# Self-attention with kept score tiles: six kept steps of eight in place of five, and the work around them set to other steps

## The chip, the cores and the metric

The kernel runs on one core of one Trainium2 chip. The metric is device time in microseconds (us) of one launch; the figure shown for a kernel is the median of its runs. A profile is taken from one separate execution. The engines are TensorE (PE in the profile, its weight loads PEld), VectorE (DVE), ScalarE (ACT), GpSimd (POOL) and SyncE (SP), which issues all DMAs here.

## The reference, cut to what matters

Four images of 256 channels and 64 x 64 places (4096 columns) go through two layers. Layer 0 is group norm, then self-attention over the 4096 places, added to the input; layer 1 is group norm, a 1 x 1 convolution to 32 channels, all 528 products of pairs of these, and a 1 x 1 convolution back to 256, added again.

```python
f = einsum('kc,bcn->bkn', Wq, gn(x)) + bq      # 32 x 4096
g = einsum('kc,bcn->bkn', Wk, gn(x)) + bk      # 32 x 4096
h = einsum('oc,bcn->bon', Wv, gn(x)) + bv      # 256 x 4096
s = einsum('bki,bkj->bij', f, g)               # 4096 x 4096
beta = softmax(s, axis=1)
x = x + gamma * einsum('bci,bij->bcj', h, beta)
y = relu(bn(einsum('bchw,oc->bohw', gn(x), w1) + b1))          # 32 channels
z = relu(bn(einsum('bhwt,ot->bohw', y[rows] * y[cols], w2) + b2))
x = x + z
```

## The kernel before, in words

The attention is worked tile by tile. A tile is 128 keys (columns j of `s`); there are 32 tiles in an image and 128 in all. Each tile takes eight steps, one for each chunk of 512 queries, in the order of `CHUNK_AT`. A step of the program has the index `u`; `t` is its place in a group of four tiles (0 to 31), `J` the group in an image (0 to 7), `b` the image (0 to 3), `s8` its place in the tile (0 to 7). All numbers are split in a high and a low half of float16, so that a step on TensorE holds eight matmuls of the high half of the powers with both halves of `h` (L1772, L1773) and, at its end, four with the low half (L1784). In between stands the score piece of a tile that is `AHEAD` = 18 steps on (L1577): 128 keys by 512 queries, from which VectorE takes the maximum.

The powers `exp(s - max)` of a step come about in one of two ways.

- **Made in place.** TensorE computes the scores again, transposed, four matmuls of 128 x 128 (`scores`, L1597), two or three steps ahead. ScalarE takes the exponential twice from PSUM (`powers`: `ph`, float16, L1333, and back to PSUM in float32, L1334), VectorE subtracts the one from the other to give the low half (`low_part`, `pl`, L896).
- **Kept.** VectorE writes the score piece to SBUF while it takes its maximum (`ks`, L863). Once the tile's maximum is known (`tile_max`, `kbias`), ScalarE takes the exponential in place (L1345); the high half `kb` is either a second exponential by ScalarE (L1343, the places in `HIGH_BY_ACT`) or a cast by VectorE (L891); GpSimd subtracts to give the low half (`kept_low`, L1162). SyncE then issues a DMA transpose of both halves into `kt` (`turn`, L521), and TensorE takes `kt` as weights.

`KEPT_STEPS` says which of the eight steps of a tile are kept, from tile 2 on. For each of them, `EXP_AT`, `CAST_AT`, `LOW_AT` and `TURN_AT` say at which step ScalarE, VectorE, GpSimd and SyncE take their part of it into their own order; steps of 8 and more are those of the tile itself, smaller ones those of the tile before. Every engine runs its own program in order, and semaphores are all that ties them; the rings `ks`, `kb` and `kt` hold 8, 4 and 5 pieces.

The three banks of the score pieces and of the other small results are used in turn: a piece on TensorE waits until VectorE has read the one two steps earlier. When a tile is done, VectorE takes the reciprocal of its sum (`invert`, in step 1 of the next tile), ScalarE divides (`divide`, L1351, `ot`), and after four tiles TensorE transposes `ot` and VectorE adds it to x (`finish`). The rest of the work (normalising chunks for the queries, keys and values of the next image, `xh` on ScalarE, L1301; the second layer of the image before: `rt`, `ql`, `qh`, `zt`) stands at fixed places `t` in the same orders. x lies in a ring of `XR` chunks; a chunk that isn't there any more is loaded again through `xt`.

Of the kernel before, what the change touches and what calls it, by code (L numbers as in the profile page):

```python
# [33 lines left out]
KEPT_STEPS = (1, 2, 4, 6, 7)  # L34
# [20 lines left out]
XR = 14  # L55
# [8 lines left out]
def build(nc, x, wq, wk, wv, w1, w2, vec, ident, gmean, sel, out):  # L64
# [5 lines left out]
    with ctx:  # L70
# [130 lines left out]
        kp_ok, kc_ok, kl_ok = sem("kp_ok"), sem("kc_ok"), sem("kl_ok")  # L201
# [39 lines left out]
        VORD = (4, 0, 5, 1, 6, 2, 3, 7)  # L241
# [206 lines left out]
        def _(sp):  # L448
# [149 lines left out]
        def _(dve):  # L598
# [252 lines left out]
            def step_piece(u):  # L851

                if u + AHEAD < ALL:
# [7 lines left out]
                    if m >= KS_RING:  # L861
                        dve.wait_ge(kl_ok, m - KS_RING + 1)
# [20 lines left out]
            def kept_high(tile, r):  # L883
# [7 lines left out]
                V.tensor_copy(kb[:, m % KB_RING, 0], ks[:, m % KS_RING]).then_inc(kc_ok, 1)  # L891

# [111 lines left out]
            def attend(b):  # L1004
                for J in range(NCH):
# [3 lines left out]
                    for t in range(NT):  # L1009
# [93 lines left out]
        def _(pool):  # L1103
# [92 lines left out]
            for b in range(B):  # L1196
# [4 lines left out]
                for J in range(NCH):  # L1201
                    G, n = b * NCH + J, (b - 1) * NCH + J
                    for t in range(NT):
# [7 lines left out]
                        for r in range(KEPT):  # L1211
                            if t % NCH == LOW_AT[r] % NCH and is_kept_tile(tile - LOW_AT[r] // NCH):
# [13 lines left out]
                        if t in (14, 17, 20, 23) and b < LASTB and J == NCH - 1:  # L1226
# [731 lines left out]
```

## Time and profile before

| | us |
|---|---|
| median of 3 runs | 2097.68 (2096.98 to 2099.1) |
| the profiled execution | 2099.17 |
| its span, first to last instruction | 2097.4 |
| TensorE busy in it | 2052.2 (98%) |
| VectorE, ScalarE, GpSimd busy | 1571.7, 1626.0, 1464.8 |

The profiled execution took 1.8 us more than its span, and 1.5 us more than the median of the runs. The granted TensorE clock is at its upper level, 2.4 GHz, in all 40 slices of the span. The busy time of a matmul counts it to its modelled end, while the next has already begun, so what a group of matmuls costs is read from the start of the one to the start of the next. ScalarE's and VectorE's instructions overlap a little too.

### The profile page before, as it was taken

The page shows a single profiled execution, that of the slowest core. Times are in us where ns is not written, and L with a number is a line of the kernel's source. Part 1 is how long each engine was busy: PE and PEld are TensorE (multiplying, and loading weights), DVE is VectorE, ACT ScalarE, POOL GpSimd, SP SyncE. Part 2 cuts the span into 40 slices and gives each one's busy share as a digit, 9 for nine tenths or more (in the row PEclk, how much of TensorE's full clock was granted, in tenths as well). Part 3 has the DMA queues.
Part 4 walks back from the last instruction along what each step waited for, and adds up shares of the span by engine and source line. Part 5 has one row for each costly group of instructions (what it writes and reads, how often), then busy time and mean ns, then how long its engine had stood idle before and what let it go on. Part 6 is the DMA issues. An engine that isn't in the chain of part 4 may idle for free.

```text
span 2097.4 us, 48084 instructions
## 1 busy us (share of the span) xinstructions
PE 2052.2 (98%) x17334; PEld 1612.2 (77%) x17334; DVE 1571.7 (75%) x3491; ACT 1626.0 (78%) x2582; POOL 1464.8 (70%) x2110
## 2 busy tenths in 40 slices
PE   4899999999999999999999999999999999999999
PEld 3688888888877777777877777777787777877854
DVE  8787877778776776877768777776877767676667
ACT  5677877778787878888778788877787777878767
POOL 3265666657677777877768687777867767677766
PEclk9999999999999999999999999999999999999999
DMA  5165777776477797778468687787837776675632
GB/s 191 37 102 96 138 143 144 139 127 118 83 133 126 146 166 150 148 149 162 90 138 144 120 162 141 155 170 138 158 78 135 146 126 138 124 137 92 140 73 80
DMA packets 728269, 271.89 MB, mean 130 GB/s; under 512 B 674240, under 2 KB 681152, under 8 KB 728000
## 3 DMA queue, kind: packets, MB, share of 16 engines
q1 hardware_dynamic: 728032, 268.82, 66.2%
q8 instruction: 138, 2.26, 0.5%
q14 instruction: 99, 0.81, 0.1%
HBM read 77.07 MB, written 19.92 MB: 46 GB/s over the span
## 4 chain that ended last, share of the span: by engine, by line
PE 92%; DVE 3%; ACT 2%; issue 1%; POOL 1%; DMA 1%; SPq 0%; DVEq 0%; ACTq 0%
PE acc L1784 21%; PE acc L1772 20%; PE acc L1773 20%; PE tps L1577 5%; PE acc L1577 5%; PE sps L1597 4%; PE tps L1648 4%; PE acc L1571 3%; PE tps L1650 2%; PE acc L1648 1%; PE tps L1612 1%; PE tps L1558 1%; PE tps L1634 1%; PE acc L1650 1%; PE sps L1547 1%
## 5 line engine op out<-in xcount | busy, mean ns | idle before, releaser
L1162 POOL TENSOR_TENSOR kb<-ks,kb 128x512 f16<-128x512 f32 x630 | 750.6, 1196 | 346.6 <-ACT ks L1345 181.8
L1772 PE MATMUL acc<-hth,kt 128*128 128x257 f16 x2520 | 587.2, 273 | 0.0
L1773 PE MATMUL acc<-htl,kt 128*128 128x256 f16 x2520 | 586.6, 273 | 0.0
L1345 ACT ACTIVATE ks<-ks,kbias,esc 128x512 f32<-128x512 f32 x630 | 506.6, 805 | 0.0
L1333 ACT ACTIVATE ph<-sps,esc 128x512 f16<-128x512 f32 x394 | 269.6, 684 | 276.2 <-PE sps L1597 263.1
L863 DVE TENSOR_SCALAR_CACHE_REDUCE ks<-acc 128x512 f32<-128x512 f32 x378 | 259.6, 687 | 180.7 <-PE acc L1577 178.2
L1784 PE MATMUL acc<-hth,kt 128*128 128x257 f16 x2520 | 385.8, 274 | 0.0
L1772 PE MATMUL acc<-hth,ph 128*128 128x257 f16 x1576 | 367.4, 274 | 0.5 <-ACT ph L1333 0.5
L1773 PE MATMUL acc<-htl,ph 128*128 128x256 f16 x1576 | 366.9, 273 | 0.0
L1784 PEld LDWEIGHTS acc<-hth,kt 128*128 128x128 f16 x2520 | 247.8, 98 | 100.6
L1343 ACT ACTIVATE kb<-ks,kbias,esc 128x512 f16<-128x512 f32 x378 | 305.5, 808 | 21.9 <-DMA kt<-kb 18.3
L849 DVE TENSOR_REDUCE mx<-tps 128x1 f32<-128x512 f32 x269 | 183.8, 686 | 152.5 <-PE tps L1577 152.4
L896 DVE TENSOR_TENSOR pl<-sps,ph 128x512 f16<-128x512 f32 x394 | 269.2, 683 | 18.5 <-ACT sps L1334 18.4
L1772 PEld LDWEIGHTS acc<-hth,kt 128*128 128x128 f16 x2520 | 247.0, 98 | 40.1 <-issue 6.2
L1773 PEld LDWEIGHTS acc<-htl,kt 128*128 128x128 f16 x2520 | 246.2, 98 | 35.5
L1334 ACT ACTIVATE sps<-sps,esc 128x512 f32<-128x512 f32 x394 | 258.1, 655 | 0.0
L1784 PE MATMUL acc<-hth,pl 128*128 128x257 f16 x1576 | 241.5, 274 | 0.6 <-DVE pl L896 0.6
L1139 POOL TENSOR_TENSOR xl<-xn,xh 128x512 f16<-128x512 f32 x176 | 210.8, 1216 | 44.6 <-DVE xn L831 27.0
L863 DVE TENSOR_SCALAR_CACHE_REDUCE ks<-tps 128x512 f32<-128x512 f32 x252 | 172.9, 686 | 52.4 <-PE tps L1577 50.2
L1784 PEld LDWEIGHTS acc<-hth,pl 128*128 128x128 f16 x1576 | 154.7, 98 | 64.5 <-DVE pl L896 2.4
L1577 PE MATMUL tps<-fst,gst 96*128 96x512 f16 x521 | 197.3, 381 | 2.6 <-DVE htl L844 0.9
L1577 PE MATMUL acc<-fst,gst 96*128 96x512 f16 x503 | 191.7, 381 | 0.0
(254 smaller groups left out, 3360.4 us busy)
## 6 DMA issues: line engine op xcount, KB each, us to landing
rt<-turned SPq DMA_DIRECT2D x96, 256.0 KB, 4.9
xt<-x SPq DMA_DIRECT2D x46, 512.0 KB, 4.4
xb<-x SPq DMA_DIRECT2D x32, 512.0 KB, 4.9
out<-zt SPq DMA_DIRECT2D x45, 256.0 KB, 2.7
kt<-kb SPq DMA_TRANSPOSE x630, 3.2
yb<-turned SPq DMA_DIRECT2D x36, 128.0 KB, 2.6
rt<-turned SPq DMA_DIRECT2D x72, 64.0 KB, 2.2
turned<-yb SPq DMA_DIRECT2D x12, 256.0 KB, 2.4
```

Source lines behind the costliest of these rows:

```text
L863: V.tensor_scalar(ks[:, m % KS_RING], pbank[par][:], 1.0, None, ALU.mult, ALU.max, accum_out=mx[:, tile % 4, PIECES[place]:PIECES[place] + ...
L896: V.tensor_tensor(pl[:, v % SLOTS], sps[v % 2][:], ph[:, v % SLOTS], ALU.subtract).then_inc(pl_ok, 1)
L1139: tt(xl[:, slot_of(job), h], xn[:, h], xh[:, slot_of(job), h], ALU.subtract).then_inc(xl_ok, 1)
L1162: tt(kb[:, m % KB_RING, 1], ks[:, m % KS_RING], kb[:, m % KB_RING, 0], ALU.subtract).then_inc(kl_ok, 1)
L1333: A(ph[:, v % SLOTS], sps[v % 2][:], ACT.Exp, scale=esc[:]).then_inc(ph_ok, 1)
L1334: A(sps[v % 2][:], sps[v % 2][:], ACT.Exp, scale=esc[:]).then_inc(p32_ok, 1)
L1343: A(kb[:, m % KB_RING, 0], ks[:, m % KS_RING], ACT.Exp, bias=kbias[:, tile % 2:tile % 2 + 1], scale=esc[:])
L1345: A(ks[:, m % KS_RING], ks[:, m % KS_RING], ACT.Exp, bias=kbias[:, tile % 2:tile % 2 + 1], scale=esc[:]).then_inc(kp_ok, 1)
L1577: fill(mm(pbank[par][:], gst[0:96, key_tile(tile)], fst[0:96, tile // NT % 2, c * CH:(c + 1) * CH], start=True, stop=True), par)
L1772: mm(bank[:, 0:C + 1], high[:, q], hth[:, c * QT + q], start=(s8 == 0 and q == 0), stop=False)
L1773: mm(bank[:, 0:C], high[:, q], htl[:, c * QT + q], start=False, stop=False)
L1784: last = mm(bank[:, 0:C + 1], low[:, q], hth[:, c * QT + q], start=False, stop=(s8 == NCH - 1 and q == QT - 1))
```

## The change

A sixth step of each tile is kept: steps 1, 2, 3, 5, 6, 7 in place of 1, 2, 4, 6, 7, so that two steps are made in place (0 and 4) and not three (0, 3, 5). VectorE casts three of the six high halves in place of two of five, and makes one of the low halves, that of the sixth piece, in step 0 (`kept_low` on VectorE, with a semaphore `kd_ok` of its own); GpSimd makes the other five. The rings grow to 9, 5 and 6 pieces and the ring of x shrinks from 14 chunks to 13. The division goes from step 4 to step 3, the transposes of the output from t = 4 and 7 to 5 and 8 with what follows them on VectorE, and the places of all parts of the kept steps and of the value chunks change.

```diff
-KEPT_STEPS = (1, 2, 4, 6, 7)
+KEPT_STEPS = (1, 2, 3, 5, 6, 7)
...
-HIGH_BY_ACT = (0, 2, 3)
-EXP_AT = (3, 4, 6, 7, 8)
-CAST_AT = (None, 3, None, None, 7)
-LOW_AT = (2, 3, 5, 7, 8)
-TURN_AT = (3, 4, 6, 8, 9)
-DIVIDE_AT = 4
-ROW_AT = 6
+HIGH_BY_ACT = (0, 2, 4)
+EXP_AT = (1, 2, 3, 5, 6, 8)
+CAST_AT = (None, 1, None, 4, None, 7)
+LOW_AT = (0, 2, 3, 5, 6, None)
+TURN_AT = (2, 3, 5, 6, 7, 9)
+LOW_BY_DVE = (5,)
+DIVIDE_AT = 3
+ROW_AT = 5
...
-KS_RING = 8
-KB_RING = 4
-KT_RING = 5
+KS_RING = 9
+KB_RING = 5
+KT_RING = 6
...
-XR = 14
+XR = 13
...
-        VORD = (4, 0, 5, 1, 6, 2, 3, 7)
+        VORD = (4, 0, 5, 3, 6, 1, 2, 7)
...
-        V_EARLY = (12, 15, 18, 21)
+        V_EARLY = (11, 15, 19, 26)
...
+            def kept_low(tile, r):
+
+                m = count_of(tile, r)
+                dve.wait_ge(kc_ok, casts_until(m))
+                V.tensor_tensor(kb[:, m % KB_RING, 1], ks[:, m % KS_RING], kb[:, m % KB_RING, 0],
+                                ALU.subtract).then_inc(kd_ok, 1)
...
+                        if s8 == 0 and is_kept_tile(tile) and (t or J):
+                            kept_low(tile, LOW_BY_DVE[0])
...
-                        if b and n >= 1 and t in (3, 4, 7, 10, 12):
-                            product_low(n - 1, (3, 4, 7, 10, 12).index(t))
-                        if J and t in (5, 8):
-                            finish(G - 1, (t - 5) // 3, 1)
-                        if J and t in (6, 11):
-                            second_stats(G - 1, (t - 6) // 5, 1)
+                        if b and n >= 1 and t in (4, 5, 8, 10, 12):
+                            product_low(n - 1, (4, 5, 8, 10, 12).index(t))
+                        if J and t in (6, 9):
+                            finish(G - 1, (t - 6) // 3, 1)
+                        if J and t in (11, 14):
+                            second_stats(G - 1, (t - 11) // 3, 1)
...
-                        if J and t in (4, 7):
+                        if J and t in (5, 8):
```

The same place of the program is shown before and after on two engines: the fourth tile of group J = 4 of image b = 1 (t = 24 to 31). In a row, `ks` written from `ks` is a kept piece's exponential, `kb` its high half, `ph` and `sps` the two exponentials of a step made in place, `ot` the division of the tile before, `gst` the copy of a row of maxima, `xh` a chunk normalised for the next image. The changed kernel's lines are 6, 13 or 17 higher than those of the kernel before (L1360 is the former L1343, L1362 the former L1345, L1350 and L1351 the former L1333 and L1334, L1368 the former L1351, L1318 the former L1301).

ScalarE before, from the powers of step 3 to those of step 5:

```order
L1333 ACTIVATE ph<-sps0,esc 128x512
L1334 ACTIVATE sps0<-sps0,esc 128x512
L1343 ACTIVATE kb<-ks,kbias,esc 128x512
L1345 ACTIVATE ks<-ks,kbias,esc 128x512
L1301 ACTIVATE xh<-xt,nbias0,rstd0 128x512 x2
L1351 ACTIVATE ot<-acc0,rinv 128x256
L1345 ACTIVATE ks<-ks,kbias,esc 128x512
L1333 ACTIVATE ph<-sps1,esc 128x512
L1334 ACTIVATE sps1<-sps1,esc 128x512
```

ScalarE now, from the first kept piece of the next tile to the powers of step 4:

```order
L1360 ACTIVATE kb<-ks,kbias,esc 128x512
L1362 ACTIVATE ks<-ks,kbias,esc 128x512
L1335 ACTIVATE qkh0<-tps1,bqk2 128x512
L1362 ACTIVATE ks<-ks,kbias,esc 128x512
L1368 ACTIVATE ot<-acc0,rinv 128x256
L1360 ACTIVATE kb<-ks,kbias,esc 128x512
L1362 ACTIVATE ks<-ks,kbias,esc 128x512
L1318 ACTIVATE xh<-xt,nbias0,rstd0 128x512 x2
L1350 ACTIVATE ph<-sps1,esc 128x512
L1351 ACTIVATE sps1<-sps1,esc 128x512
```

The powers of step 3 are gone; the division has moved ahead of the third kept piece and of the normalised chunk, and all of these stand ahead of the powers of step 4.

VectorE before, from the low half for step 0 to the first cast after the reciprocal (`mx` is a piece's maximum, `ks,mx` that of a kept piece, `qkl0` queries and keys of the next image, `rinv` the reciprocal):

```order
L896 TENSOR_TENSOR pl<-sps1,ph 128x512
L891 CAST kb<-ks 128x512
L839 SCALAR_TENSOR_TENSOR qkl0<-tps1,bqk2,qkh0 128x512
L849 TENSOR_REDUCE mx<-acc3 128x1
L849 TENSOR_REDUCE mx<-tps0 128x1
L902 RECIPROCAL rinv<-acc0 128x1
L863 TENSOR_SCALAR ks,mx<-acc3 128x512
L896 TENSOR_TENSOR pl<-sps0,ph 128x512
L863 TENSOR_SCALAR ks,mx<-tps0 128x512
L891 CAST kb<-ks 128x512
```

VectorE now, at the same place:

```order
L909 TENSOR_TENSOR pl<-sps0,ph 128x512
L897 CAST kb<-ks 128x512
L845 SCALAR_TENSOR_TENSOR qkl0<-tps1,bqk2,qkh0 128x512
L855 TENSOR_REDUCE mx<-acc3 128x1
L903 TENSOR_TENSOR kb<-ks,kb 128x512
L869 TENSOR_SCALAR ks,mx<-tps0 128x512
L915 RECIPROCAL rinv<-acc0 128x1
L897 CAST kb<-ks 128x512
L869 TENSOR_SCALAR ks,mx<-acc3 128x512
L869 TENSOR_SCALAR ks,mx<-tps0 128x512
L909 TENSOR_TENSOR pl<-sps1,ph 128x512
```

The sixth piece's low half (L903) now stands ahead of the reciprocal, a cast behind it, and one low half from PSUM is gone. Over the whole program TensorE has 504 matmuls of scores fewer; VectorE has 126 casts and 126 low halves of kept pieces more, 126 low halves from PSUM fewer, and 126 plain maxima have become maxima with a copy; ScalarE has 126 exponentials of kept pieces more and 252 others fewer; GpSimd has as many instructions of each kind as before; SyncE has 126 DMA transposes more and 5 loads into `xt` more.

## Rows read from the trace of the kernel before

**Rows 1.** The page, part 1: span; engine, busy us, share, instructions.

```profile
span 2097.4 us, 48084 instructions
...
PE 2052.2 (98%) x17334; PEld 1612.2 (77%) x17334; DVE 1571.7 (75%) x3491; ACT 1626.0 (78%) x2582; POOL 1464.8 (70%) x2110
```

**Rows 2.** Waits of TensorE, 135 to 2010 us: us in total, times, longest.

```profile
PE sps L1597 <- ACT gst L1326: 1.3, 2, 0.9
PE tps L1577 <- DVE htl L844: 0.9, 3, 0.3
PE tps L1577 <- DVE ks L863: 0.8, 3, 0.4
PE acc L1784 <- DVE pl L896: 0.6, 3, 0.2
```

**Rows 3.** Busy time by stretch: engines, then granted clock, DMA share, GB/s.

```profile
140.00:230.00 90.00, 90.00 (x805) 75.22 (x803) 74.36 (x193) 68.25 (x110) 52.19 (x95) 1.00 0.61 108
...
848.00:908.00 60.00, 60.00 (x512) 47.21 (x511) 45.85 (x101) 49.12 (x78) 49.04 (x70) 1.00 0.85 154
```

**Rows 4.** Timeline of TensorE, 817 to 823 us: start, us, line, tiles.

```profile
817.58 0.27 PE L1772 MATMUL acc<-hth,ph 128*128 128x257 f16 x1
...
818.45 0.38 PE L1577 MATMUL tps<-fst,gst 96*128 96x512 f16 x1
...
819.13 0.27 PE L1772 MATMUL acc<-hth,kt 128*128 128x257 f16 x1
...
820.67 0.39 PE L1597 MATMUL sps<-gst,fst 128*128 128x128 f16 x4
820.90 0.27 PE L1772 MATMUL acc<-hth,kt 128*128 128x257 f16 x1
```

**Rows 5.** Groups by line, whole span: count, busy us, mean ns, idle before.

```profile
L1345 ACT ACTIVATE ks<-ks,kbias,esc 128x512 f32<-128x512 f32 x630 | 506.6, 805 | 0.0
...
L1333 ACT ACTIVATE ph<-sps,esc 128x512 f16<-128x512 f32 x394 | 269.6, 684 | 276.2 <-PE sps L1597 263.1 <-PE acc L1784 8.1
...
L891 DVE CAST kb<-ks 128x512 f16<-128x512 f32 x252 | 131.7, 522 | 10.3 <-DMA kt<-kb 4.8 <-ACT ks L1345 4.5
...
L946 DVE SCALAR_TENSOR_TENSOR ql<-qh,rt 128x512 f16<-128x512 f16 x92 | 88.2, 959 | 0.0
```

**Rows 6.** Timeline of ScalarE, 818 to 824 us.

```profile
818.93 0.81 ACT L1343 ACTIVATE kb<-ks,kbias,esc 128x512 f16<-128x512 f32 x1
...
820.34 1.51 ACT L1301 ACTIVATE xh<-xt,nbias,rstd 128x512 f16<-128x512 f32 x2
821.75 0.46 ACT L1351 ACTIVATE ot<-acc,rinv 128x256 f32<-128x256 f32 x1
822.11 0.81 ACT L1345 ACTIVATE ks<-ks,kbias,esc 128x512 f32<-128x512 f32 x1
822.81 0.68 ACT L1333 ACTIVATE ph<-sps,esc 128x512 f16<-128x512 f32 x1
823.38 0.65 ACT L1334 ACTIVATE sps<-sps,esc 128x512 f32<-128x512 f32 x1
```

**Rows 7.** Single lines of VectorE: duration ns min/median/max.

```profile
L946 DVE SCALAR_TENSOR_TENSOR ql<-qh,rt x92: 676/684/1755, 597.4 to 1980.5; 128x512 f16<-128x512 f16 x92
...
L891 DVE CAST kb<-ks x252: 408/421/1486, 96.5 to 2001.5; 128x512 f16<-128x512 f32 x126
...
L896 DVE TENSOR_TENSOR pl<-sps,ph x394: 673/685/692, 70.5 to 2004.8; 128x512 f16<-128x512 f32 x197
```

**Rows 8.** Transposes issued from 140 to 230 us.

```profile
L521 SPq DMA_TRANSPOSE kt<-kb x33: 1232/1232/2566, 140.0 to 228.9; - x33
...
DMA to landing us min/median/max: 3.0/3.1/4.9
```

**Rows 9.** Timeline of VectorE, 818 to 820 us.

```profile
818.87 0.69 DVE L849 TENSOR_REDUCE mx<-tps 128x1 f32<-128x512 f32 x1 [0.45 <-PE tps L1577]
819.48 0.16 DVE L902 RECIPROCAL rinv<-acc 128x1 f32<-128x1 f32 x1
```

More of the change, by code:

```diff
@@ L200, in build @@
         kbias_ok = sem("kbias_ok")
-        kp_ok, kc_ok, kl_ok = sem("kp_ok"), sem("kc_ok"), sem("kl_ok")
+        kp_ok, kc_ok, kl_ok, kd_ok = sem("kp_ok"), sem("kc_ok"), sem("kl_ok"), sem("kd_ok")
         kt_in = [sem(f"kt_in{i}") for i in range(KT_RING)]
@@ L289, in build @@
         STATS.update({at: (2 + i // NCH, i % NCH) for i, at in enumerate(LATER_STATS)})
-        V_EARLY = (12, 15, 18, 21)
+        V_EARLY = (11, 15, 19, 26)
         def in_place(b, c):
-            return b == 0 or (c < XR - NCH if b == 1 else c < 4)
+            return b == 0 or (c < XR - NCH if b == 1 else c < 3)
         USED = {}
@@ L412, in casts_until, with low_done @@
             return sum(k % KEPT not in HIGH_BY_ACT for k in range(m + 1))
+        def low_done(m):
+            own = m % KEPT in LOW_BY_DVE
+            return (kd_ok if own else kl_ok), sum((k % KEPT in LOW_BY_DVE) == own for k in range(m + 1))
         def kept_step(m):
@@ L517, in turn @@
                 m = count_of(tile, r)
-                sp.wait_ge(kl_ok, m + 1)
+                sp.wait_ge(*low_done(m))
                 if m >= KT_RING:
@@ L1051, in attend @@
                             normed(("qk", b + 1, 2 * (J - 2)))
-                        if b < LASTB and J == NCH - 1 and t in (13, 16, 19, 22):
-                            normed(("v", b + 1, VORD[(13, 16, 19, 22).index(t)]))
+                        if b < LASTB and J == NCH - 1 and t - 1 in V_EARLY:
+                            normed(("v", b + 1, VORD[V_EARLY.index(t - 1)]))
             project()
@@ L1211, in _ @@
                         for r in range(KEPT):
-                            if t % NCH == LOW_AT[r] % NCH and is_kept_tile(tile - LOW_AT[r] // NCH):
+                            if LOW_AT[r] is not None and t % NCH == LOW_AT[r] % NCH and is_kept_tile(tile - LOW_AT[r] // NCH):
                                 kept_low(tile - LOW_AT[r] // NCH, r)
@@ L1225, in _ @@
                             low(("qk", b + 1, 2 * (J - 3) + 1))
-                        if t in (14, 17, 20, 23) and b < LASTB and J == NCH - 1:
-                            low(("v", b + 1, VORD[(14, 17, 20, 23).index(t)]))
+                        if t - 2 in V_EARLY and b < LASTB and J == NCH - 1:
+                            low(("v", b + 1, VORD[V_EARLY.index(t - 2)]))
                         if t == 20 and b and 1 <= n < SHARED - 1:
@@ L1456, in attend @@
                             high(("qk", b + 1, 2 * (J - 2)))
-                        if b < LASTB and J == NCH - 1 and t in (12, 15, 18, 21):
-                            high(("v", b + 1, VORD[(12, 15, 18, 21).index(t)]))
+                        if b < LASTB and J == NCH - 1 and t in V_EARLY:
+                            high(("v", b + 1, VORD[V_EARLY.index(t)]))
             act.wait_ge(set_dve, mark["scaled_qkv"])
```

14 lines of the change are left out of this document (8 added, 6 removed).

## The prediction

> **What bounds the kernel now.** I read the page's first part first: TensorE is busy 98% of the span, the other three engines 70 to 78% [rows 1]. Busy time of matmuls is modelled, so the list of TensorE's waits comes second: between 135 and 2010 us, where the attention runs, it waited four kinds of times, 1.3 + 0.9 + 0.8 + 0.6 = 3.6 us together [rows 2]. The clock is granted in full (1.00, that is 2.4 GHz) in the stretches I read [rows 3]. So in these 1875 us the time is the number of matmuls by their pitch, and nothing else ends last. The timeline gives the pitch: a step from the first matmul of its high halves to that of the next is 1.55 us (817.58 to 819.13), and four matmuls of scores add 0.23 us where they stand (820.67 to 820.90, both rounded) [rows 4].
>
> **What the change removes.** In each of the 126 tiles from tile 2 on, one step more is kept, and its four matmuls of scores go; the order shows all 504 gone and nothing put in their place, because the piece that VectorE now also copies was computed before anyway. Other such pairs in the timeline print 0.22 us, so I take 0.22: 126 x 0.22 = **27.7 us**, all on the path, since TensorE hardly waits. From above the gain is bounded by this and the 3.6 us of present waits, 31.3 us. From below nothing bounds it but what the other engines give back, which is the rest of this part.
>
> **ScalarE** loses two exponentials of a tile (684 ns, and 0.65 us in its timeline) and gets one (805 ns) [rows 5, 6], 0.53 us less in a tile of some 13 to 15 us. It gains nothing on the path.
>
> **VectorE** gets a cast more (522 ns in the mean) [rows 5], and a low half from SBUF in place of one from PSUM. The trace has no such subtraction with both inputs in SBUF on this engine; the nearest row is `ql`, which reads two: 684 ns in the median and 1755 at most, where the low half from PSUM never takes over 692 [rows 7], and 959 in the mean [rows 5]. So it costs from nothing to 1.07 us more than what it replaces; I take the mean's 0.28. That makes 0.52 to 1.59 us a tile, 0.80 as taken. In the busiest stretch VectorE idles 60.00 - 45.85 = 14.15 us over four tiles [rows 3], 3.5 us a tile. On average it fits; where it stands in the order is weighed below.
>
> The cast shows the same spread, 408 to 1486 ns [rows 7]. The Trainium skill, "SBUF — State Buffer", section "Who interferes with whom", has a rule for it: a VectorE instruction with two SBUF inputs, or a cast in a two-port mode, shares a port pair with GpSimd, and the second to start blocks until the first is done. This trace agrees: of the three lines shown, the two of these kinds alone have long ones, by up to 1.08 us. By the rule the new low half would be blocked in the worst case in every tile; by the row's mean it loses 0.28 us.
>
> **GpSimd** has as many instructions as before. **SyncE** issues four transposes more in a group of four tiles, 1.23 us each [rows 8]: 24 x 1.23 = 29.6 us of some 59, besides a few dozen short issues. **The DMA engines** are the tighter place. From 140 to 230 us they were 0.61 busy [rows 3] with 33 transposes issued [rows 8]: 0.61 x 90 / 33 = 1.66 us of all engines for one, an upper bound, as other loads are in it. The busiest group that I read has 0.85 x 60 = 51.0 us [rows 3]; four more make 57.6 of the 59.1 us that it would last. That is 97%, and still below the path. The five more loads of x are spread over the images; I count them at nothing, covered by the groups with a lower share, and at most at two transposes' time (3.3 us) each if that cover is gone.
>
> **The moves.** The division now stands in step 3, ahead of the third kept piece, and the powers of step 4 stand behind both. This is a chain that begins at the end of the last tile. I count from the first matmul of a tile (817.58). Its score piece starts at +0.87 [rows 4]; VectorE reads it from +1.29 and has the reciprocal at +2.06, having idled 0.45 us before it [rows 9]. The new low half stands ahead, 0.68 us, 0.23 more than that idle time: +2.29. The division takes 0.36 us until the next instruction starts, so it ends at +2.65; two exponentials of a kept piece take 1.41 (818.93 to 820.34): +4.06; `ph` is done 0.68 later [rows 6], at +4.74. TensorE wants it after four steps and one set of scores, 4 x 1.55 + 0.22 = +6.42. `sps` starts 0.57 after `ph` and takes 0.65 [rows 6], so it ends at +5.28, its low half (0.68) at +5.96; TensorE wants that at 6.42 + 0.87 + 0.22 = +7.51. In a plain tile the margins are thus 1.7 and 1.5 us. At t = 27 of groups 2 to 5 of the first three images, and at t = 11 and 19 of their last group, a normalised chunk (1.41 us) [rows 6] stands in between: 18 places with margins of 0.3 and 0.1 us. There one mean delay of VectorE (0.28) is felt, and what waits behind the late powers is TensorE itself. I charge 0.3 us to each, 18 x 0.3 = **5 us**; with no delay it would be 0, with the full 1.07 it would be 18 x 0.9 = 16 us.
>
> Behind the same exponentials stands a wait for a free place of `kb`: the third piece's needs the landing of the fourth piece of the tile before. That one may be issued when its slot is free, two steps (3.1 us) before the tile ends, and lands 3.1 us later [rows 8], at about 0; ScalarE comes there at +2.65. This cover ends when landing takes over 5.7 us. The transposes of the output at t = 5 start some 5 us after the division's end and cost nothing; the maxima and copies of the sixth piece have the chain's usual time, since its transpose can be issued once the low half is there (about +1.6), and its use is in step 7 (+11.1).
>
> **Sum.** On the profiled execution's span: 2097.4 - 27.7 + 5 = 2074.7 us. It took 1.8 us more than its span and 1.5 us more than the median of the runs: 2074.7 + 1.8 - 1.5 = **2075.0 us**.
>
> **The rivals.**
>
> *Half given back at VectorE.* From step 7 to step 1 it has a cast, the low half and the second cast close together, and pieces behind them that TensorE needs read within two steps. If the delays by GpSimd hit often, TensorE waits in plain tiles too. For it: three casts and a low half in a tile can each be held up to 1.07 us, against a margin of 1.5. Against it: 3.5 us of idle time in a tile, and 0.28 in the mean. From 0.22 us a tile it eats the whole gain. At 0.15 us, 126 x 0.15 = 19 us: 2097.7 - 27.7 + 19 = **2089 us**; up to 0.2 us, 2095. The rule of the Trainium skill named above, taken as a certain loss, would end here.
>
> *The DMA queue becomes the bound: slower.* The transposes of a group share the engines with the second layer's transfers and the loads; at 97% a burst isn't worked off, landings pass 5.7 us, `kb` and `kt` come late, and ScalarE stands with the powers behind them. For it: 0.85 already, and a landing of 4.9 us against 3.0 even in a stretch at 0.61 [rows 3, 8]. Against it: TensorE has no wait for a landing now [rows 2], and the rings grew with the pieces. If the engines can't be fuller than 0.91, midway between 0.85 and 0.97, such a group lasts 57.6 / 0.91 = 63.3 us, 4.2 more than 59.1. In the 14 later groups of images 1 and 2 that is 59 us: 2129; in half of them 2099. I price it at the middle of the two, **2114 us**. It decides from 2 us a group over those 14.
>
> *No wait at all:* 2097.7 - 27.7 = 2070 us. This is the lower part of the forecast's own range. That the change doesn't do what it says is excluded by the order, which shows the matmuls gone.
>
> **How the numbers follow.** The forecast, with 0 to 16 us given back and up to 3.6 us of old waits gone, runs from 2066 to 2086: 0.72. Half given back at VectorE (2086 to 2097): 0.16. The DMA queue: 0.12. Within 0.2% (4.2 us, about what a measurement of this kernel can tell from no change) is 2093.5 to 2101.9. Faster: 0.72 and half of the VectorE case, 0.80. Same: 0.07 of the VectorE case and 0.02 of the DMA case, 0.09. Slower: the rest, 0.11. The range reaches from 2066 into the VectorE case, to 2094, and leaves out 0.19.
>
> **What would show it.** Right: 1072 matmuls of scores, TensorE's waits in the attention still below 10 us, most of them for powers or low halves in step 4 at the 18 places; ScalarE waiting for the reciprocal ahead of the division in most tiles; VectorE's new subtraction at 0.7 to 1.2 us in the mean. Wrong: waits of TensorE for `kt`, or landings beyond 6 us in the groups of images 1 and 2 (the DMA case); waits for `ks` and `mx`, the readers of the pieces, in every tile (the VectorE case); groups of four tiles that are not 0.9 us shorter than before.

## The result and the profile after

The changed kernel takes 2186.65 us in the median of 4 runs (2182.15 to 2191.24), the kernel before 2098.39 beside it: 1.042 times as long, with an interval of 1.0389 to 1.0451. The forecast was 2075.0, at most 2094. The profiled execution took 2190.91 us, its span is 2188.8.

TensorE is busy longer than in [rows 1] although 504 matmuls have gone, and its share fell from 98 to 94%: the last matmul ahead of each wait is counted to its modelled end, and some of the work ran at half clock (last section). Part 1 of the page:

```profile
PE 2061.1 (94%) x16830; PEld 1572.5 (72%) x16830; DVE 1697.2 (78%) x3743; ACT 1575.5 (72%) x2456; POOL 1533.5 (70%) x2110
```

TensorE's waits between 141 and 2104 us, which answer to the 3.6 us of [rows 2], come to some 85 us. The largest, and that for landings (in total, times, longest):

```profile
PE acc L1789 <- ACT ph L1350: 28.4, 21, 2.5
PE tps L1594 <- DVE ks L869: 15.5, 29, 1.3
PE acc L1594 <- DVE ks L869: 13.8, 22, 1.7
PE acc L1594 <- DVE mx L855: 10.4, 7, 3.7
PE tps L1629 <- DVE xb L923: 7.8, 16, 0.6
PE acc L1789 <- DMA kt<-kb: 2.2, 3, 1.1
```

Powers come late (L1350) and pieces are read late (L869, L855); a landing ends hardly any wait of TensorE. One engine back it is otherwise. ScalarE's waits over the whole span:

```profile
ACT ot L1368 <- DVE rinv L915: 305.7, 114, 6.9
ACT kb L1360 <- DMA kt<-kb: 121.2, 55, 5.8
ACT kb L1360 <- DVE kbias L887: 68.2, 67, 2.7
```

The first two of them before the change:

```profile
ACT ot L1351 <- DVE rinv L902: 24.4, 29, 6.9
ACT kb L1343 <- DMA kt<-kb: 18.3, 12, 4.5
```

And VectorE waits for ScalarE's second power with the pieces behind it, 128.9 us in 102 waits, longest 4.4.

The groups that answer to [rows 5, 7], single lines of VectorE (count, ns min/median/max): its casts reach as far as before, `ql` far further, and the new subtraction (L903) takes 0.88 us in the mean, where the one it replaces never took over 692 ns:

```profile
L959 DVE SCALAR_TENSOR_TENSOR ql<-qh,rt x92: 677/1042/3985, 620.6 to 2072.4; 128x512 f16<-128x512 f16 x92
L897 DVE CAST kb<-ks x378: 399/426/1357, 91.4 to 2092.3; 128x512 f16<-128x512 f32 x189
L903 DVE TENSOR_TENSOR kb<-ks,kb x126: 674/682/1642, 106.0 to 2092.9; 128x512 f16<-128x512 f32 x126
```

**Where the time went.** I took the start of every score piece in both traces and compared the steps. Where nothing else is going on, the step shortens as forecast: groups 2, 4 and 6 of image 3 are 0.8 us shorter each. The loss is in the groups with odd `J` of images 1 and 2 (66 us of the 91 between the traces) and in image 0 (19), at four places above all: t = 3 and 4 (17 us of the 66), 5 to 8 (18), 24 to 26 (14) and 27 (9); another 9 lie at t = 10 to 12.

The sixth group of image 1 shows the first two and what follows them. It begins (score piece of t = 0) at 834.37 us before and at 866.91 after. First the kernel before, t = 4 to 8, 8 to 12 and 18 to 24 (columns: window, its us, busy us and instructions of PE, PEld, DVE, ACT, POOL, granted clock, DMA share, GB/s):

```profile
841.27:848.35 7.08, 7.08 (x67) 5.98 (x65) 6.57 (x14) 5.26 (x10) 6.53 (x12) 1.00 0.92 191
848.35:854.82 6.47, 6.47 (x60) 5.38 (x58) 6.17 (x15) 6.42 (x12) 6.47 (x7) 1.00 0.41 76
...
867.59:878.90 11.31, 11.31 (x101) 8.66 (x99) 6.51 (x17) 7.50 (x13) 7.82 (x15) 1.00 1.25 186
```

VectorE idled 0.51 and 0.30 us in the first two stretches, and 4.80 in the last. The window of [rows 3] began at 848 us, which is t = 8 of this group; nearly all of its 3.5 idle us a tile lay behind t = 12. After the change, t = 0 to 4, 4 to 8, 8 to 12 and 18 to 24:

```profile
866.91:875.32 8.41, 6.64 (x59) 5.29 (x57) 3.19 (x9) 4.03 (x7) 3.70 (x4) 1.00 0.70 133
875.32:886.26 10.94, 8.20 (x66) 5.87 (x64) 9.65 (x17) 9.07 (x15) 9.98 (x15) 1.00 1.10 209
886.26:894.30 8.04, 6.99 (x60) 5.10 (x57) 8.04 (x15) 4.27 (x8) 8.04 (x7) 1.00 0.40 71
...
907.23:918.32 11.09, 11.09 (x97) 8.43 (x95) 6.93 (x18) 7.63 (x12) 8.29 (x14) 1.00 1.14 199
```

The last stretch gained its 0.22 us. The second lost 3.86 (10.94 against 7.08), the third 1.57, and in the third VectorE has no idle time at all. The first, in which VectorE worked for 3.19 us only, lost 1.51. The timelines show why. SyncE's queue first:

```profile
853.88 2.01 SPq L518 DMA_DIRECT2D rt<-turned  x4
855.99 4.89 SPq L527 DMA_TRANSPOSE kt<-kb  x2
...
868.27 1.57 SPq L527 DMA_TRANSPOSE kt<-kb  x1
```

Four loads of 256 KB, and behind them two transposes in 4.89 us, where one of [rows 8] takes 1.23 to issue. From there to 868.27 the queue has no gap (eight loads of 32 KB, one of 512 KB and a transpose, not shown), and SyncE waits for no other engine. The four loads are not new: the kernel before issues them too, from 819.72 us on, ahead of this group. ScalarE:

```profile
868.14 0.47 ACT L1368 ACTIVATE ot<-acc,rinv 128x256 f32<-128x256 f32 x1 [2.96 <-DVE rinv L915]
871.77 0.81 ACT L1360 ACTIVATE kb<-ks,kbias,esc 128x512 f16<-128x512 f32 x1 [3.15 <-DMA kt<-kb]
872.49 0.80 ACT L1362 ACTIVATE ks<-ks,kbias,esc 128x512 f32<-128x512 f32 x1
873.19 0.61 ACT L1394 ACTIVATE qh<-rt 128x512 f16<-128x512 f32 x1
873.71 0.67 ACT L1350 ACTIVATE ph<-sps,esc 128x512 f16<-128x512 f32 x1
874.28 0.64 ACT L1351 ACTIVATE sps<-sps,esc 128x512 f32<-128x512 f32 x1
```

It waits 2.96 us for the reciprocal, then 3.15 for a free place of `kb`, and the powers of step 4 stand behind both. By these rows the second wait decides here: the place comes free when the transpose issued at 868.27 has landed (at 871.68), however early the reciprocal is. TensorE gets the powers 1.77 us late (its two later waits come from the next view):

```profile
874.43 0.28 PE L1789 MATMUL acc<-hth,ph 128*128 128x257 f16 x1 [1.77 <-ACT ph L1350]
...
880.71 0.39 PE L1594 MATMUL tps<-fst,gst 96*128 96x512 f16 x1 [0.85 <-DVE ks L869]
...
883.50 0.39 PE L1594 MATMUL acc<-fst,gst 96*128 96x512 f16 x1 [1.06 <-DVE ks L869]
```

VectorE stood 3.61 us for the second power, and then has to make up for it beside GpSimd's products:

```profile
874.95 0.69 DVE L909 TENSOR_TENSOR pl<-sps,ph 128x512 f16<-128x512 f32 x1 [3.61 <-ACT sps L1351]
...
877.30 1.07 DVE L897 CAST kb<-ks 128x512 f16<-128x512 f32 x1 [1.05 <-ACT ks L1362]
878.29 1.76 DVE L959 SCALAR_TENSOR_TENSOR ql<-qh,rt 128x512 f16<-128x512 f16 x1
879.97 0.68 DVE L869 TENSOR_SCALAR_CACHE_REDUCE ks<-tps 128x512 f32<-128x512 f32 x1
...
880.58 2.25 DVE L959 SCALAR_TENSOR_TENSOR ql<-qh,rt 128x512 f16<-128x512 f16 x1
882.75 0.68 DVE L869 TENSOR_SCALAR_CACHE_REDUCE ks<-acc 128x512 f32<-128x512 f32 x1
```

A cast and two `ql` take 5.08 us, and each piece that waits behind one of the `ql` is a wait of TensorE.

At t = 24 and 25 the wait for a place of `kb` reaches TensorE by another way. In the fourth group of image 2 ScalarE stands for it, the high half of the next queries and keys (`qkh`) is late with it, and VectorE stands for that, with the maximum behind it for which TensorE then waits longest (3.75 us, last section):

```profile
1322.95 0.81 ACT L1360 ACTIVATE kb<-ks,kbias,esc 128x512 f16<-128x512 f32 x1 [5.85 <-DMA kt<-kb]
...
1324.37 0.67 ACT L1335 ACTIVATE qkh<-tps,bqk 128x512 f16<-128x512 f32 x1
...
1325.08 0.75 DVE L845 SCALAR_TENSOR_TENSOR qkl<-tps,bqk,qkh 128x512 f16<-128x512 f32 x1 [4.07 <-ACT qkh L1335]
```

### The profile page after: what moved, and what is told of

Read it like the earlier page. It is cut to its first block, busy times and chain, and to the rows that moved or that the text cites. A ratio compares the mean times of both kernels' runs of the same rounds, so it can differ in the third digit from the quotient of the medians.

```text
span 2188.8 us, 47585 instructions
## 1 busy us (share of the span) xinstructions
PE 2061.1 (94%) x16830; PEld 1572.5 (72%) x16830; DVE 1697.2 (78%) x3743; ACT 1575.5 (72%) x2456; POOL 1533.5 (70%) x2110
## 3 DMA queue, kind: packets, MB, share of 16 engines
q1 hardware_dynamic: 862448, 304.48, 72.8%
## 4 chain that ended last, share of the span: by engine, by line
PE 48%; DVE 14%; issue 8%; ACT 7%; DMA 6%; POOL 5%; SPq 4%; DVEq 0%; ACTq 0%; POOLq 0%
PE acc L1801 10%; PE acc L1789 10%; PE acc L1790 10%; DMA kt<-kb 6%; DVE ks L869 4%; DVE ql L959 3%; POOL kb L1179 3%; PE acc L1594 3%; PE tps L1594 3%; PE acc L1588 3%; PE tps L1665 2%; ACT ks L1362 2%; SPq L527 2%; PE acc L1665 1%; DVE kb L897 1%
## 5 line engine op out<-in xcount | busy, mean ns | idle before, releaser
L1789 PE MATMUL acc<-hth,kt 128*128 128x257 f16 x3024 | 707.5, 274 | 2.2 <-DMA kt<-kb 2.2
L1790 PE MATMUL acc<-htl,kt 128*128 128x256 f16 x3024 | 706.4, 273 | 0.0
L1362 ACT ACTIVATE ks<-ks,kbias,esc 128x512 f32<-128x512 f32 x756 | 597.3, 804 | 3.3
L1801 PE MATMUL acc<-hth,kt 128*128 128x257 f16 x3024 | 464.2, 275 | 0.0
L1360 ACT ACTIVATE kb<-ks,kbias,esc 128x512 f16<-128x512 f32 x378 | 304.6, 806 | 190.0 <-DMA kt<-kb 121.2
L1801 PEld LDWEIGHTS acc<-hth,kt 128*128 128x128 f16 x3024 | 297.5, 98 | 120.4 <-issue 0.6
L1789 PEld LDWEIGHTS acc<-hth,kt 128*128 128x128 f16 x3024 | 297.1, 98 | 53.1 <-issue 9.9
L869 DVE TENSOR_SCALAR_CACHE_REDUCE ks<-tps 128x512 f32<-128x512 f32 x378 | 258.5, 684 | 97.8 <-PE tps L1594 96.4
L869 DVE TENSOR_SCALAR_CACHE_REDUCE ks<-acc 128x512 f32<-128x512 f32 x378 | 257.7, 682 | 62.2 <-PE acc L1594 61.1
L909 DVE TENSOR_TENSOR pl<-sps,ph 128x512 f16<-128x512 f32 x268 | 183.5, 685 | 129.3 <-ACT sps L1351 128.9
L1368 ACT ACTIVATE ot<-acc,rinv 128x256 f32<-128x256 f32 x128 | 60.4, 472 | 305.8 <-DVE rinv L915 305.7
L1789 PE MATMUL acc<-hth,ph 128*128 128x257 f16 x1072 | 251.0, 275 | 28.8 <-ACT ph L1350 28.4
L897 DVE CAST kb<-ks 128x512 f16<-128x512 f32 x378 | 223.2, 591 | 59.4 <-ACT ks L1362 38.0
L1790 PE MATMUL acc<-htl,ph 128*128 128x256 f16 x1072 | 250.7, 274 | 0.0
L1350 ACT ACTIVATE ph<-sps,esc 128x512 f16<-128x512 f32 x268 | 181.9, 679 | 24.9 <-PE sps L1614 15.6
L1351 ACT ACTIVATE sps<-sps,esc 128x512 f32<-128x512 f32 x268 | 174.3, 650 | 0.0
L1200 POOL TENSOR_TENSOR rt<-rt,yb 128x512 f32<-128x512 f32 (+1 forms) x120 | 162.6, 1367 | 16.4 <-DMA rt<-turned 16.4
```

What stands on the lines that cost most here:

```text
L869: V.tensor_scalar(ks[:, m % KS_RING], pbank[par][:], 1.0, None, ALU.mult, ALU.max, accum_out=mx[:, tile % 4, PIECES[place]:PIECES[place] + ...
L909: V.tensor_tensor(pl[:, v % SLOTS], sps[v % 2][:], ph[:, v % SLOTS], ALU.subtract).then_inc(pl_ok, 1)
L1350: A(ph[:, v % SLOTS], sps[v % 2][:], ACT.Exp, scale=esc[:]).then_inc(ph_ok, 1)
L1360: A(kb[:, m % KB_RING, 0], ks[:, m % KS_RING], ACT.Exp, bias=kbias[:, tile % 2:tile % 2 + 1], scale=esc[:])
L1362: A(ks[:, m % KS_RING], ks[:, m % KS_RING], ACT.Exp, bias=kbias[:, tile % 2:tile % 2 + 1], scale=esc[:]).then_inc(kp_ok, 1)
L1789: mm(bank[:, 0:C + 1], high[:, q], hth[:, c * QT + q], start=(s8 == 0 and q == 0), stop=False)
```

## The experiments

Three theories stood at the start. Theory 1: the order on ScalarE (division, third piece, powers of step 4). Theory 2: VectorE's load and its locks with GpSimd. Theory 3: the places of the rings and the landings. All times are medians, with the ratio to the kernel before of the same batch (its medians lie between 2097.22 and 2098.69). Experiments 5, 6, 13, 14 and 18 alter the kernel before, the others the changed kernel.

**e1: division and third piece back to step 4.**

```diff
-EXP_AT = (1, 2, 3, 5, 6, 8)
-DIVIDE_AT = 3
+EXP_AT = (1, 2, 4, 5, 6, 8)
+DIVIDE_AT = 4
```

> The changed kernel with the division back in step 4 and the third kept piece's exponentials moved from step 3 to step 4, so that the powers of step 4 stand ahead of both on ScalarE. Theory 1 (the chain from the reciprocal through the division and the third piece to the powers of step 4 holds TensorE): TensorE's waits for powers, 28.4 us, fall below 5 us, the late steps at t = 3 and 4 and t = 27 go, 2150 to 2165 us. Theory 2 (VectorE held by GpSimd): only the 1.5 to 2.8 us at t = 3 go where VectorE was not late itself, 2175 to 2187. Theory 3 (landings of transposes and a ring of 5 for six pieces): ScalarE's wait for landings stands ahead of the powers of step 4 no more, the waits at t = 24 stay, 2165 to 2180.

Measured: 2159.35, 1.0292 [1.0262, 1.0322], 27.3 below the changed kernel. ScalarE's waits for the reciprocal fall from 305.7 to 47.9 us, TensorE's for powers from 28.4 to 3.8, and the loss at t = 27 is gone. At t = 3 and 4, 11.6 of the 17.1 us stay, where theory 1 had them go. Theory 1 holds, for about a quarter of the gap to the forecast.

**e2: all six low halves on GpSimd.**

```diff
-LOW_AT = (0, 2, 3, 5, 6, None)
-LOW_BY_DVE = (5,)
+LOW_AT = (1, 2, 3, 5, 6, 8)
+LOW_BY_DVE = ()
```

> The changed kernel with all six low halves made by GpSimd (places 1, 2, 3, 5, 6, 8), none by VectorE. Theory 2 (VectorE is held because its two-input instructions and casts collide with GpSimd's): VectorE has 126 x 0.88 = 111 us less, its waits and TensorE's for pieces fall, 2150 to 2175 us; GpSimd has 126 x 1.24 = 156 us more and may be late with transposes in the odd groups. Theory 1: the reciprocal comes 0.7 us sooner in each tile, powers of step 4 too, about 2165. Theory 3: the later low half delays the sixth transpose, the waits for landings grow, 2190 to 2220.

Measured: 2174.7, 1.0365 [1.0323, 1.0407], 12 below: the upper edge of theory 2's range, with an interval that overlaps that of the changed kernel (1.0389 to 1.0451).

**e3: GpSimd's products on 64 of 512 columns** (the second layer's products are left out elsewhere).

```diff
-tt(rt0[0:rows, grp], rt0[0:rows, grp], yb0[0:rows, :], ALU.mult)
+tt(rt0[0:rows, grp, 0:64], rt0[0:rows, grp, 0:64], yb0[0:rows, 0:64], ALU.mult)
```

> The changed kernel with GpSimd's products of the second layer made on 64 of 512 columns only (the rest is left out), so that GpSimd is out of VectorE's way at t = 27 to 31 and 0 to 4 of the odd groups. Theory 2: the two subtractions ql at t = 4 and 5, 1.76 and 2.25 us in an odd group, fall to 0.68 each, and with them the 2.7 us that the steps t = 5 to 7 lose in every odd group from J = 3 on (some 10 groups), 2145 to 2165 us. Theories 1 and 3: nothing but GpSimd's own lateness goes, 2175 to 2187.

Measured: 2179.57, 1.0388 [1.0358, 1.0418], 7 below, and the intervals overlap here too. The loss at t = 5 of the odd groups goes, that at 7 and 8 stays: being held up by the products is a small part, and theory 2's number is missed.

**e4: seven places of `kb`** (12 chunks of x to make room).

```diff
-KB_RING = 5
-XR = 13
+KB_RING = 7
+XR = 12
```

> The changed kernel with a ring of 7 pieces for kb in place of 5; the room comes from the ring of x, 12 chunks in place of 13 (a few more loads through xt, one place of the statistics moved by two steps). Theory 3: ScalarE's wait for landings, 121 us in 55 places, falls below 30 us; the late steps at t = 24 and 25 go, 2150 to 2170 us. Theories 1 and 2: ScalarE then waits for the reciprocal in the same places, 2175 to 2190.

Measured: 2163.14, 1.031 [1.028, 1.034], 23.5 below, although image 0 gets 6.6 us longer (ScalarE waits 25.0 us for chunks of x). Its waits for a place of `kb` are gone. In the odd groups of images 1 and 2 the loss at t = 24 falls from 10.8 to 1.0 us, and that at t = 3 and 4 from 17.1 to nothing, with the order on ScalarE as it was. Theory 3 holds too.

**e5: the kernel before with the scores of step 3 computed twice.**

```diff
-for q in range(QT):
+for q in tuple(range(QT)) * (2 if tile >= FIRST_TILE and u % NCH == 3 else 1):
```

> The kernel before (five kept steps) with the four matmuls of scores of step 3 issued twice in each tile from tile 2 on: 126 sets more, nothing else. If a set of scores lies wholly on the path, as the prediction's term of 27.7 us has it: 2098 + 28 = 2126 us. If TensorE hides a part of it, less, down to 2098.

Measured: 2125.28, 1.0128 [1.0099, 1.0158]: 27.1 us for 126 sets of scores. The price of a set is as the forecast had it.

**e6: the kernel before with 13 chunks of x**, loaded in the changed kernel's order (`XR`, `VORD`, `V_EARLY`).

> The kernel before with the ring of x at 13 chunks in place of 14, and the order and the places of the value chunks that go with it; five kept steps as before. If the shorter ring and the five more loads cost nothing, as the prediction counts them: 2096 to 2100 us. If they hold the transposes up in SyncE's queue or the DMA engines: 2105 to 2120, with the loss at the loads.

Measured: 2102.79 (8 runs), 1.0026 [1.0014, 1.0038]: 4.6 us, two thirds of it in the sixth group of image 0.

**e7: e1 and e4 together.**

> The changed kernel with both remedies: the division and the third piece in step 4 (first experiment) and a ring of 7 for kb with 12 chunks of x (fourth). If the two losses are apart, the gains add up: 27 + 23 us, 2136 us. If both only moved the same wait, about 2160. Theory 2 says that what is left (some 38 us over the kernel before) stands at t = 5 to 13, on VectorE.

Measured: 2157.89, 1.0284 [1.0254, 1.0313]. The two don't add. In the odd groups of images 1 and 2, of 66 us lost, 48 are left in e1, 32 in e4 and 31 in e7. In image 0 the 12 chunks eat e1's gain: ScalarE now waits 43 us for chunks of x, up to 13.4 at once. And t = 5 to 8 loses nearly as before (15.2 us against 17.9).

**e8: e7 with the products' low halves (`ql`) at their old places.**

```diff
-if b and n >= 1 and t in (4, 5, 8, 10, 12):
+if b and n >= 1 and t in (3, 4, 7, 10, 12):
```

> As the one before, with VectorE's five subtractions ql (product_low) back at t = 3, 4, 7, 10, 12, from 4, 5, 8, 10, 12. Theory 2: the pair of them beside GpSimd's products is what costs 2.7 us in an odd group; at t = 3 and 4 they meet the products no less, so little changes at the first two (2130 to 2140), but the one at t = 7 leaves the step with the sixth piece's low half, and 1 to 2 us a group go at t = 8 to 12: 2115 to 2130 in all.

Measured: 2137.36, 1.0186 [1.0156, 1.0215], 20.5 below e7; t = 7 of the odd groups loses 1.7 us where it lost 7.9. A move of one step of three subtractions, which the forecast doesn't mention, is worth 20 us.

**e9 to e12: e1 and the old places of `ql`, with the room shared out otherwise.**

```diff
 e9   KB_RING = 6   KT_RING = 5   KS_RING = 9   XR = 13
 e10  KB_RING = 6   KT_RING = 6   KS_RING = 8   XR = 13
 e11  KB_RING = 5   KT_RING = 5   KS_RING = 8   XR = 14   and VORD, V_EARLY as before
 e12  as e9, LOW_AT = (1, 2, 3, 5, 6, 8), LOW_BY_DVE = ()
```

> The division and the third piece's exponentials back in step 4, the products' low halves back at t = 3, 4, 7, 10, 12, six places of kb, five of kt, 13 chunks of x. Theory 1 (the order on ScalarE and VectorE, the five places of kb and the chunks of x cost separately what they measured so far): 2159 - 20 for the low halves - 10 to 20 for the sixth place of kb: 2117 to 2130. Rival (the fewer places of kt only move the wait for a landing from kb to kt): 2139 or above, with ScalarE's waits for kb short and SyncE's for TensorE long.

> The same, with the place taken from ks (eight) and not from kt (six). Theory 1: 2117 to 2130 again. If the places of ks matter (VectorE's piece waits for the low half of eight pieces before), 2139 or above, with VectorE's waits ahead of the pieces longer.

> Division and third piece in step 4 and the products' low halves back, with 14 chunks of x in their old order, so that eight places of ks and five each of kb and kt are left. If the five more loads cost what they cost the kernel before (4.6 us): 2130 to 2137, with the stretch behind the turned chunks (t = 24 to 26) as long as in the changed kernel. If the loads are what makes the landings late there: below 2125, and that stretch is shorter by half.

> As the first of these four, with all six low halves on GpSimd, none on VectorE. If VectorE's new low half is what is left at t = 5 to 8: 10 to 15 us below the first (2105 to 2118), as it was 12 us in the changed kernel. If the delay is GpSimd's own (it then has one more subtraction of 1.2 us a tile): no gain, 2117 to 2135.

Measured: e9 2144.16, 1.022 [1.019, 1.025]; e10 2146.28, 1.023 [1.0201, 1.026]; e11 2215.48, 1.056 [1.0524, 1.0597]; e12 2138.88, 1.0195 [1.0145, 1.0245]. Theory 1's 2117 to 2130 is missed in both e9 and e10. Against the 2139 that their expectations start from (e1 less 20 for `ql`, not run by itself), taking a place from `kt` or `ks` costs at least what the sixth place of `kb` brings: in e9 SyncE waits 433.8 us for TensorE to free a place of `kt` (243.6 in the changed kernel), in e10 VectorE's pieces wait 92.1 us for a low half. e11 is far off both expectations: the rings of the kept pieces, not the chunks of x, are where room is worth most in this kernel. ScalarE waits 213.1 us for landings in it, in 98 waits.

e12 against e9 can't be told apart, since their intervals overlap.

**e13, e14, e18: the kernel before with one extra thing a tile**, on a constant piece and a place that nobody reads, in the room of the fourteenth chunk of x (so they compare with e6, 2102.79): a transpose (e13), a cast and a subtraction from SBUF on VectorE (e14), the cast alone (e18).

```diff
+if t % NCH == 5 and is_kept_tile(tile):                                          # e13, SyncE
...
+    sp.dma_start_transpose(dk[:], dz[:].rearrange("p e n -> p (e n)")).then_inc(d_in, 16)
...
+if s8 == 0 and is_kept_tile(tile) and (t or J):                                   # e14, VectorE
...
+    V.tensor_tensor(dd[:, 1], ds[:], dd[:, 0], ALU.subtract).then_inc(d_ok, 1)
+if s8 == 4 and is_kept_tile(tile + 1):                                            # e14 and e18
...
+    V.tensor_copy(dd[:, 0], ds[:]).then_inc(d_ok, 1)                              # e14
+    V.tensor_copy(dd[:, tile % 2], ds[:])                                         # e18
```

> The kernel before with 13 chunks of x (2102.8 alone) and one transpose more in each tile, of a constant piece into a place that nobody reads: 126 transposes on SyncE's queue and the DMA engines, no work for any other engine. If the transposes themselves delay the landings of the others (the DMA theory): 2115 to 2150, with ScalarE's waits for kt's landings, 0 before, at 30 us or more. Rival (the engines have room, and only the rings and the order of the changed kernel make its landings late): 2103 to 2110, with few such waits.

> The kernel before with 13 chunks of x (2102.8 alone) and one cast and one subtraction from SBUF more in each tile on VectorE, of a constant piece into a place that nobody reads: about 1.4 us a tile, 0.6 more than the change adds. If VectorE's load is the rest: 2115 to 2140, with TensorE's waits for ks and mx, 1 us or so before, above 10. If its idle time of 3.5 us a tile takes them, as the forecast had it: 2103 to 2110.

> The kernel before with 13 chunks of x (2102.8 alone) and one cast more in each tile on VectorE, in step 4, of a constant piece into a place that nobody reads: about 0.87 us a tile. If VectorE's load alone at the change's size costs: half of e14's 43 us or more, 2120 to 2135, at t = 5 of the odd groups. If the subtraction at the tile's first step (ahead of the reciprocal and the pieces) is what cost in e14: 2103 to 2112.

Measured: e13 2115.83, 1.0083 [1.0066, 1.01], 13.0 above e6; e14 2145.48, 1.0223 [1.0208, 1.0238], 42.7 above; e18 2128.86, 1.015 [1.0134, 1.0167], 26.1 above. e13's expectation has a wrong number: ScalarE waited 18.3 us for landings before, not 0; in e6 it is 12.0, in e13:

```profile
ACT kb L1354 <- DMA kt<-kb: 48.9, 33, 4.8
```

e18 shows theory 2's mechanism by itself. One cast of 0.89 us in the mean costs TensorE 0.21 us a tile, at t = 5 above all (against the kernel before, 9.7 us in the odd groups of images 1 and 2, 4.5 in image 3), and VectorE is busy 1675.5 us against 1570.7 in e6, 104.8 more where the change brought 125.5. How much of the changed kernel's own loss this makes is not shown by it. Its timeline of VectorE at t = 3 to 5 of the same group as above:

```profile
850.00 0.69 DVE L898 TENSOR_TENSOR pl<-sps,ph 128x512 f16<-128x512 f32 x1
850.60 1.35 DVE L1027 CAST dd<-ds 128x512 f16<-128x512 f32 x1
851.88 2.88 DVE L948 SCALAR_TENSOR_TENSOR ql<-qh,rt 128x512 f16<-128x512 f16 x1
854.68 0.68 DVE L865 TENSOR_SCALAR_CACHE_REDUCE ks<-tps 128x512 f32<-128x512 f32 x1
```

In the kernel before no such cast stands there, and the next piece starts 2.14 us after `pl` (at 840.33), where in e18 it is 4.68:

```profile
840.93 1.62 DVE L946 SCALAR_TENSOR_TENSOR ql<-qh,rt 128x512 f16<-128x512 f16 x1
842.47 0.68 DVE L863 TENSOR_SCALAR_CACHE_REDUCE ks<-tps 128x512 f32<-128x512 f32 x1
```

A cast of 0.42 us at its median [rows 7] thus makes a delay of 2.54 here, since both it and the `ql` behind it are stretched. Load and stretching are not told apart by this run.

**e15: e12 with the four large loads of a turned group at 64 of 512 columns** from the second on (the second layer then works on old numbers).

> The kernel with division and third piece in step 4, old places of the products' low halves, all low halves on GpSimd and six places of kb (2138.9), in which the four large loads of the turned groups bring 64 of 512 columns from the second on (the second layer then works on old numbers). If these loads make the landings late behind them: the loss at t = 24 to 26 goes (7 us in that kernel) and the total falls by 7 to 15, 2124 to 2132. If transposes are late for their own number: within 4 us of 2139.

Measured: 2105.04, 1.0027 [1.0014, 1.0041], 34 below e12. More than expected: not only t = 24 (7.4 to 1.0 us) but t = 5 (7.1 to 0.9) and 4 (6.4 to 3.5) shrink, the places behind the loads of the odd and of the even groups. In the kernel before the same loads stand beside 3.6 us of TensorE's waits [rows 2], so there they cost next to nothing.

**e16, e17: e12 with the cast of the second piece given to ScalarE; e17 also issues those loads apart.**

```diff
-HIGH_BY_ACT = (0, 2, 4)
+HIGH_BY_ACT = (0, 1, 2, 4)
...
-if odd and t == 17:
-    rotate_groups(n)
+if odd and t in (17, 19, 21, 23):
+    rotate_groups(n, ((t - 17) // 2,))
```

> The kernel of 2138.9 (division and third piece in step 4, old places of the products' low halves, all low halves on GpSimd, six places of kb), in which ScalarE writes the high half of the second kept piece with an exponential of its own, in place of VectorE's cast: four pieces by ScalarE, two by VectorE as in the kernel before. If VectorE's load is what is left: the waits behind VectorE's pieces at t = 4 to 9 go, 2110 to 2125. If it is the landings (ScalarE waits 145 us for them there): within 5 us of 2139, or above, since ScalarE has 0.1 us a tile more to do than before.

> The same with the four 256 KB loads of a turned group issued two steps apart (odd groups) or one step apart (even groups, but in the first group of an image) in place of together. If a burst of loads is what holds the landings: 10 to 25 us below e16, toward 2097 or less. If it is the number of bytes, in whatever order: within 5 us of e16.

Measured: e16 2151.56, 1.0263 [1.0217, 1.031]; e17 2127.51, 1.0142 [1.0125, 1.0159]. The same bytes in another order are worth 24 us, as expected: the burst holds the landings. ScalarE's waits for them are 142.0 us in e16 and 57.1 in e17. In e16 VectorE is relieved of a cast and nothing is won, which falls on the side of the landings: its median is 13 us above e12, but its runs reach from 2145 to 2168 and the intervals overlap. e17 has the lowest median of the kernels with six kept pieces that do all the work, and is still 29 us above the kernel before.

## Why the prediction was wrong

**The step that failed** is the one on VectorE: "On average it fits", from 3.5 us of idle time a tile. The load itself was sized well: 1697.2 - 1571.7 = 125.5 us more, 1.00 us a tile against 0.80 as taken and 0.52 to 1.59 as bounded, though 28.0 of the 125.5 us are `ql`, which got longer and wasn't counted. But idle time was averaged over a window that began at t = 8 and ended in quiet steps. It was not the busiest stretch either: from 140 to 230 us VectorE idled 90.00 - 74.36 = 15.64 us [rows 3], 2.4 a tile. In t = 4 to 12 it had 0.81 us in 13.55, so added work has hardly anywhere to go there. Measured alone, in the kernel before: 26 us for the cast, 43 with a subtraction (which in the change takes the place of one of 0.68 us, so its share there is smaller). The rival "half given back at VectorE" had this mechanism and priced it at 19.

**The chain (right mechanism, far too small).** The forecast put the reciprocal at +2.29 us of a tile, from one tile, and charged 5 us at 18 places. Over 125 tiles of the trace after, from a tile's first matmul (its first score piece less 0.87) to the reciprocal's end, the median is 3.76 us at t = 8, 3.31 at 16, 2.47 at 24 and 2.07 at 0, the longest 7.78; before it was 2.05 to 2.27. Ahead of it stand VectorE's new load and pieces that TensorE itself brings late (in the group shown, VectorE waits 1.33 us for the piece ahead of the reciprocal). TensorE waited 28.4 us for powers; e1 puts the order's price at 27. A part of this it shares with the next term: at t = 3 and 4 the wait for `kb` ends last, and e4 takes that loss away without touching the order.

**The cover of the `kb` wait.** "This cover ends when landing takes over 5.7 us" looked at the landing alone. The transpose must first be issued, in SyncE's order, behind large loads and other transposes: in the group shown it was issued at 868.27 and had landed by 871.77, 3.5 us later, and still held ScalarE 3.15 us. ScalarE waited 55 times, 121.2 us, with a median landing of 3.3 us on the page. Two places more were worth 23.5 (e4), the burst of loads 24 to 34 (e15, e17). That is the rival of the DMA queue, at less than a full queue: 72.8% of the span for the kernel's queue. It too was priced lower than it came, at 2114, and a full queue is not what it takes: in the kernel before it was 92.6% busy from 823 to 840 us, where TensorE hardly waited. For the four more transposes of a group, which the forecast's sum puts at nothing, e13 measured 13.0 us; for the loads of x, counted "at nothing", e6 measured 4.6.

**Left out.** The moves of `ql` to t = 4, 5 and 8 weren't costed: 20 us (e8). Neither were the second transposes of the output (L1629), which waited 7.8 us for VectorE.

**What held.** 27.7 us for the scores (27.1 in e5); ScalarE waiting for the reciprocal in most tiles (114); the new subtraction at 0.88 us in the mean, within the 0.7 to 1.2 named; waits for `ks` and `mx` as the mark of the VectorE case, though 58 of them and not one in every tile.

The Trainium skill, "SBUF — State Buffer", section "Who interferes with whom", has an exclusive lock, issue order deciding who blocks. The prediction used it with a loss of at most 1.07 us; this trace agrees with the lock and not with that bound: `ql` reached 3.98 us.

The prices don't add to the 112 us between forecast and result, and shouldn't: a late landing makes ScalarE late, that makes VectorE late, and VectorE then has no idle time to make it up, so each cure takes away part of what another would. e7 shows that directly for the order and the places of `kb`. A remainder stays open: with the order and the places of `ql` undone, and in e12 the new low half too, e9 and e12 are still 45 and 40 us above the kernel before. Cutting the loads' bytes takes 34 us off e12, and the extra transposes, measured apart in the kernel before, cost 13; that the two together are the remainder is not shown.

## What to carry to other kernels

Read an engine's room from the stretch in which the added work stands, step by step, never from a window that averages it with quieter ones; then ask the trace how long each instruction queued behind it may wait. When a ring has fewer places than one tile has pieces, its cover includes the time that the freeing DMA stands in the issuing queue, and one burst of large loads can take it all. Before betting on a trade between engines, add the new load alone to the old kernel, as e18 does: that one run would have warned that 27 us of matmuls might be bought for 26 us of one cast.

## What the runs showed of the hardware

A VectorE instruction with two inputs in SBUF can stand for several GpSimd instructions. The longest `ql` of the changed kernel, which takes 0.68 us at its shortest, and GpSimd beside it:

```profile
620.57 3.98 DVE L959 SCALAR_TENSOR_TENSOR ql<-qh,rt 128x512 f16<-128x512 f16 x1
```

```profile
619.10 2.68 POOL L1200 TENSOR_TENSOR rt<-rt,yb 128x512 f32<-128x512 f32 x2
621.74 2.26 POOL L1179 TENSOR_TENSOR kb<-ks,kb 128x512 f16<-128x512 f32 x2
```

It ends at 624.55, 0.55 us after the last of these four, three of which ran beside it (the second begins at 620.33). Where `ql` begins first it is GpSimd that is longer: beside a `ql` of 0.68 us at 634.01, GpSimd's subtraction of 634.08 takes 1.63 us, where the two above take 2.26 together.

The longest wait cost TensorE twice. Windows of the changed kernel around its longest wait (window, its us, PE busy, granted clock, DMA share, GB/s), and the matmuls behind it:

```profile
1322.00:1326.40 4.40, 0.73 (x7) 0.85 0.94 217
1326.40:1330.40 4.00, 3.92 (x17) 0.50 0.55 95
1330.40:1340.00 9.60, 9.60 (x75) 0.92 0.58 130
```

```profile
1326.48 0.61 PE L1594 MATMUL acc<-fst,gst 96*128 96x512 f16 x1 [3.75 <-DVE mx L855]
1326.88 1.07 PE L1801 MATMUL acc<-hth,kt 128*128 128x257 f16 x4
```

After these 3.75 us without work the clock is granted at 0.50, that is 1.2 GHz, and the score piece takes 0.61 us in place of 0.38. Over the span the mean clock is 0.995 where it was 1.000: if that is time at half clock, it is by this estimate 0.01 x 2189 = 22 us of it, and some 11 us of the loss.
